# Second half of a four-layer network on one core: four attentions of layer 2 ahead of the first of layer 3, other planned times for the networks' steps, another buffer for the last residual rows

## The reference, cut to what matters

```
x += attn0(norm(x), ctx, ctx, causal)      ; x += norm(x) @ sign(W)
x += attn1(norm(x), ctx, ctx, causal)      ; x += mixture(norm(x))      # 16 experts, top 2, and 2 shared
x += attn2(ctx, norm(x), mask)             ; x += quantised(norm(x))    # silu(gate)*up, down; ternary weights, 8-bit rows
x += attn3(norm(x), ctx, ctx)              ; x += blocks(norm(x))       # below
blocks(h): 3 times  h = lin(gelu(norm(lin(h)) * g + b)) + h
```

## Time and profile before

| | us |
|---|---|
| median of 3 runs | 1590.66 (1587.65 to 1593.19) |
| the profiled execution | 1588.46 |
| its span, first to last instruction | 1586.6 |
| TensorE busy in the span | 1236.1 (78%) |
| VectorE busy | 970.9 (61%) |
| ScalarE busy | 834.0 (53%) |
| GpSimd busy | 434.1 (27%) |
| mean granted TensorE clock | 0.892 of 2.4 GHz |

### The profile page before, as it was taken

One profiled execution on the slowest core, in us unless ns is written; L12 is line 12 of the kernel. 1 busy time (PEld: TensorE's weight loads), 2 busy tenths in 40 slices (PEclk: granted clock), 3 DMA queues, 4 the chain that ended last, 5 costly groups with the idle time before them and its releaser, 6 DMA issues.

```text
span 1586.6 us, 26659 instructions
## 1 busy us (share of the span) xinstructions
PE 1236.1 (78%) x9430; PEld 903.2 (57%) x9430; DVE 970.9 (61%) x2625; ACT 834.0 (53%) x1554; POOL 434.1 (27%) x943
## 2 busy tenths in 40 slices
PE   2888888888998969777887778678686786866775
PEld 2666676666777857655665545446364563543543
DVE  2556765555555658665666777676676856757521
ACT  3445545443555545444554635657466574755651
POOL 3001131444233372444223143212132121111222
PEclk8899999889999989888999969799898897987886
DMA  8566643345776454342856734332243312333000
GB/s 219 134 140 144 96 94 54 54 68 107 146 176 155 115 111 89 79 74 90 180 136 167 170 103 80 40 55 36 31 67 40 56 28 37 41 53 40 1 7 14
DMA packets 98210, 140.06 MB, mean 88 GB/s; under 512 B 12320, under 2 KB 79520, under 8 KB 98080
## 3 DMA queue, kind: packets, MB, share of 16 engines
q1 hardware_dynamic: 90048, 105.58, 36.2%
q0 software_dynamic: 8032, 32.78, 7.6%
HBM read 65.43 MB, written 22.54 MB: 55 GB/s over the span
## 4 chain that ended last, share of the span: by engine, by line
PE 42%; DVE 21%; ACT 13%; POOL 10%; issue 8%; DMA 5%; SPq 1%; ACTq 0%; DVEq 0%; POOLq 0%
PE ps L845 12%; PE ps L959 4%; PE ps L853 4%; PE ps L1049 3%; PE ps L867 3%; PE ps L887 3%; DVE bn L1328 3%; DVE neg_max L1448 2%; POOL rstd L1759 2%; PE ps L837 2%; ACT xn L1181 2%; PE ps L1015 2%; DMA x_rows<-xn,dest 2%; ACT probs L1224 1%; ACT L1311 1%
## 5 line engine op out<-in xcount | busy, mean ns | idle before, releaser
L1224 ACT ACTIVATE probs<-ps 128x384 f32<-128x384 f32 (+1 forms) x512 | 274.2, 542 | 308.9 <-PE ps L890 110.7
L867 PE MATMUL ps<-k_st,q_st 96*128 96x256 bf16 (+1 forms) x1024 | 231.0, 278 | 44.2 <-issue 14.5
L1448 DVE TENSOR_REDUCE neg_max<-ps 128x2 f32<-128x512 f32 x256 | 172.7, 682 | 138.6 <-PE ps L867 81.0
L1756 POOL TENSOR_SCALAR var_eps<-mv 128x2 f32<-128x2 f32 x112 | 25.9, 232 | 845.4 <-DVE mv L1331 842.4
L887 PE MATMUL ps<-q_st,k_st 104*128 104x256 bf16 (+1 forms) x1024 | 229.3, 277 | 21.2 <-ACT q_st L1236 17.7
L1445 DVE TENSOR_REDUCE tri<-ps 128x3 f32<-128x384 f32 x256 | 139.7, 552 | 154.8 <-PE ps L870 153.3
L1236 ACT ACTIVATE q_st<-ps 8x1024 bf16<-8x1024 f32 x128 | 130.2, 1017 | 52.8 <-PE ps L941 50.0
L959 PE MATMUL ps<-probs,v 128*32 128x256 f32 (+1 forms) x2048 | 137.9, 391 | 22.3 <-ACT probs L1224 20.8
L887 PEld LDWEIGHTS ps<-q_st,k_st 104*128 104x128 bf16 x1024 | 103.3, 104 | 66.9 <-ACT q_st L1236 25.2
L867 PEld LDWEIGHTS ps<-k_st,q_st 96*128 96x128 bf16 x1024 | 106.1, 105 | 61.5 <-issue 30.5
L870 PE MATMUL ps<-diag_s,ident_b 128*128 128x128 bf16 x512 | 107.5, 232 | 0.0
(11 more groups left out here) (245 smaller groups left out, 2695.9 us busy)
## 6 DMA issues: line engine op xcount, KB each, us to landing
k_st<-parts SPq DMA_DIRECT2D x192, 128.0 KB
q_st<-parts SPq DMA_DIRECT2D x192, 128.0 KB, 6.8
x_rows<-wo SPq DMA_DIRECT2D x10, 768.0 KB, 8.6
ctx_t<-in_ctx_t SPq DMA_DIRECT2D x16, 256.0 KB, 7.3
ring<-x_rows SPq DMA_DIRECT2D x31, 128.0 KB, 3.5
y_rows<-ring SPq DMA_DIRECT2D x31, 128.0 KB, 3.2
xn_t<-x_rows SPq DMA_DIRECT2D x31, 128.0 KB, 3.8
y_rows<-vec SPq DMA_DIRECT2D x31, 128.0 KB, 3.8
```

Of the source, the lines that this page charges most:

```text
L867: last = mm(t[:, c0:c0 + n], head(q_st, r, h, KROWS, j * P, P), head(k_st, r, h, KROWS, 0, n), start=True, stop=L == 3)
L1224: nc.scalar.activation(probs[:, (hg % 2) * HPG + h4, 0:width], tile_of(key)[:, 0:width], ACT.Exp, scale=SCALE).then_inc(*tile_drained(key))
L1448: V.tensor_reduce(neg_max[:, hg, h4, :], tile_of(key).rearrange("p (j t) -> p j t", j=SJ), AX.X, ALU.max, negate=True).then_inc(*tile_drai ...
```

## The change

1. `interleave(2, 3, 4)`: the second half becomes (2,0) (2,1) (2,2) (2,3) (3,0) (2,4) (3,1) (2,5) (3,2) (2,6) (3,3) (2,7) (3,4) (3,5) (3,6) (3,7). Layer 3 of batch b starts at least four slots after layer 2 of b; before it was three for batches 0 and 7.
2. In the lanes of the second half the offsets are longer: the norm 3.0/4.8/5.8 becomes 4.0/6.6/7.6, a hidden step 8.0 becomes 12.0, a block 18.6 becomes 24.0. `TIME` stays at 42.
3. The lane of the queries of layer 2 starts 1.65 slots ahead of its attention and not 2.
4. The expert tiles of the second group are planned 2.8 apart and not 3.2, so `LOW_AT` and what hangs on it move earlier; the lora weights come after mask 4 and not after mask 3.
5. The contexts of batches 4 to 7 for layer 2 are loaded at a planned time 4.0 into the slot before layer 3 of b - 4.
6. The residual rows of batches 6 and 7 are kept in `stage`, the masks' buffer, loaded once the last mask is made; the alternate y buffers go to batches 5 and 7.

```diff
-HALVES = (list(FIRST), interleave(2, 3))
+HALVES = (list(FIRST), interleave(2, 3, 4))
-TILE_STEP = (3.5, 3.2)
+TILE_STEP = (3.5, 2.8)
+LORA_AT = max(LOW_AT, START[2, 2] + TIME[1] + 2.0) + 2.0
 def norm(part, p, b, t):
+    wait = (3.0, 4.8, 5.8) if p[1] in "01" else (4.0, 6.6, 7.6)
-NORM = 7.0
-OUT = 12.4
+NORM = (7.0, 9.6)
+OUT = (12.4, 13.6)
 def project(part, L, b):
+    wait = (1.4, 2.6, 5.0) if L < 2 else (1.4, 3.6, 6.0)
 def loads_second(part, b):
-    yield START[2, b] - 3.0 * TIME[1]
+    yield START[2, b] - 3.0 * TIME[1] if b < 4 else START[3, b - 4] - TIME[1] + 4.0
 def masks_second(part, b):
-    t = 50.0 + 20.0 * b if b < 2 else max(j - 1.65 * T, START[2, b - 2] + T + 2.0)
-    if b > 3:
-        t = max(t, LOW_AT + 56.0)
+    t = 50.0 + 20.0 * b if b < 2 else START[2, b - 2] + T + 2.0
+    if b > 4:
+        t = max(j - 1.65 * T, t, LORA_AT + 60.0)
 def query_second(part, b):
-    t = START[2, b] - 2 * TIME[1]
+    t = START[2, b] - 1.65 * TIME[1]
-    yield t + 9.4
+    yield t + 12.0
     part.token_bias("q", b)
-    yield t + 13.4
+    yield t + 17.0
     part.apply("q", b)
 def between_second(part, b):
-    yield t + 8.8
+    yield t + 11.4
     part.quantised(b)
...
-        T, s = b * SJ + a, t + 11.2 + 8.0 * a
+        T, s = b * SJ + a, t + 14.4 + 12.0 * a
-            yield s + 2.6 * c
+            yield s + 4.0 * c
             part.hidden(T, c)
...
-        yield s + 2.8
+        yield s + 4.0
         part.down(T)
...
-    t += 35.4
+    t = max(t + 48.0, k - 3.0)
     yield t
     part.ln("l3a", b)
...
 def after_second(part, b):
-    t = START[3, b] + TIME[1] + 6.6
+    t = START[3, b] + TIME[1] + 7.2
-        s = t + NORM + 18.6 * n
+        s = t + NORM[1] + 24.0 * n
...
-        yield s + 6.2
+        yield s + 7.4
         part.apply(("y", n), b)
-        yield s + 8.0
+        yield s + 10.4
         part.block_turn(n, b)
-        yield s + 9.2
+        yield s + 11.4
         part.block_gelu(n, b)
-        yield s + 12.4
+        yield s + 16.0
         part.block_out(n, b)
-        yield s + 14.8
+        yield s + 18.4
         part.block_add(n, b)
-            yield s + 16.0
+            yield s + 20.6
             part.h_turn(n + 1, b)
...
         def y_set(b):
-            return y_sets[1 if b == B - 2 else 0]
+            return y_sets[1 if b in (B - 3, B - 1) else 0]
         def h_of(b):
-            return ctx_n[:, b % 3, :, :]
+            if b < B - 2:
+                return ctx_n[:, b % 3, :, :]
+            return stage[:, (b - B + 2) * SJ * D:(b - B + 3) * SJ * D].rearrange("p (a d) -> p a d", a=SJ)
...
                 def ctx_load(b):
-                    if b > 2:
+                    if b == B - 2:
+                        sp.wait_ge(*mask_ready.at((B - 1, 1)))
+                    elif 2 < b < B - 2:
                         wait_drained(sp, ("z", NBLK - 1, b - 3))
                 def mask_load(b):
-                    elif b == NB:
+                    elif b == NB + 1:
                         wait_drained(sp, ("lora", 2 * NBLK - 1))
                 def lora_load(n):
-                        sp.wait_ge(*mask_ready.at((NB - 1, 1)))
+                        sp.wait_ge(*mask_ready.at((NB, 1)))
```

More of the change, by code:

```diff
@@ L181, in norm @@
 def norm(part, p, b, t):
+    wait = (3.0, 4.8, 5.8) if p[1] in "01" else (4.0, 6.6, 7.6)
     yield t
     part.ln(p, b)
-    yield t + 3.0
+    yield t + wait[0]
     part.apply(p, b)
-    yield t + 4.8
+    yield t + wait[1]
     part.turn(p, b)
-    yield t + 5.8
+    yield t + wait[2]
     part.turned(p, b)
-NORM = 7.0
-OUT = 12.4
+NORM = (7.0, 9.6)
+OUT = (12.4, 13.6)
 def before_first(part, b):
@@ L208, in project @@
     t = START[L, b] + time_of(L) + 6.2
+    wait = (1.4, 2.6, 5.0) if L < 2 else (1.4, 3.6, 6.0)
     yield t
     part.project_in(L, b)
-    yield t + 1.4
+    yield t + wait[0]
     part.projected(L, b)
-    yield t + 2.6
+    yield t + wait[1]
     part.project_out(L, b)
-    yield t + 5.0
+    yield t + wait[2]
     part.project_add(L, b)
 def between_first(part, b):
-    t = START[0, b] + TIME[0] + OUT
+    t = START[0, b] + TIME[0] + OUT[0]
     yield from project(part, 0, b)
     yield from norm(part, "l0f", b, t)
-    yield t + NORM
+    yield t + NORM[0]
     part.ffn0(b)
-    yield t + NORM + 2.4
+    yield t + NORM[0] + 2.4
     part.ffn0_add(b)
-    yield from norm(part, "l1a", b, t + NORM + 3.2)
+    yield from norm(part, "l1a", b, t + NORM[0] + 3.2)
     yield from stacks(part, 1, b)
 def after_first(part, b):
-    t = START[1, b] + TIME[0] + OUT
+    t = START[1, b] + TIME[0] + OUT[0]
     yield from project(part, 1, b)
     yield from norm(part, "l1f", b, t)
-    t += NORM
+    t += NORM[0]
     yield t
@@ L262, in shared_experts @@
 def shared_experts(part, b):
[L264 removed]
+    s = START[1, b] + TIME[0] + OUT[0] + NORM[0] + 2.0
     yield s
@@ L448, in between_second @@
         part.down_copy(T)
-        yield s + 2.8
+        yield s + 4.0
         part.down(T)
-        yield s + 4.2
+        yield s + 5.4
         part.down_add(T)
-    t += 35.4
+    t = max(t + 48.0, k - 3.0)
     yield t
     part.ln("l3a", b)
-    yield t + 3.0
+    yield t + 4.0
     part.apply("l3a", b)
-    yield max(k + 0.6, t + 3.2)
+    yield k + 0.6
     part.k_hi(3, b)
-    yield max(k + 1.8, t + 3.6)
+    yield k + 1.8
     part.k_rest(3, b)
-    yield max(k + 4.6, t + 4.8)
+    yield max(k + 4.6, t + 6.6)
     part.turn("l3a", b)
-    yield max(k + 5.8, t + 5.8)
+    yield max(k + 5.8, t + 7.6)
     part.q_hi(3, b)
-    yield max(k + 6.8, t + 6.8)
+    yield max(k + 7.2, t + 9.0)
     part.q_rest(3, b)
-    yield max(k + 9.0, t + 9.0)
+    yield max(k + 9.4, t + 11.2)
     part.v_take(3, b)
 def after_second(part, b):
-    t = START[3, b] + TIME[1] + 6.6
+    t = START[3, b] + TIME[1] + 7.2
     yield from norm(part, "l3f", b, t)
     for n in range(NBLK):
-        s = t + NORM + 18.6 * n
+        s = t + NORM[1] + 24.0 * n
         yield s
@@ L747, in build @@
         ctx_in = [signal(f"ctx_in{r}", 16) for r in range(4)]
-        ctxn_in = [signal(f"ctxn_in{r}", 16) for r in range(3)]
+        ctxn_in = [signal(f"ctxn_in{r}", 16) for r in range(4)]
         mask_in = signal("mask_in", 16)
@@ L1965, in ctx_load @@
                         wait_drained(sp, ("v", 1, B - 1))
-                    if b > 2:
+                    if b == B - 2:
+                        sp.wait_ge(*mask_ready.at((B - 1, 1)))
+                    elif 2 < b < B - 2:
                         wait_drained(sp, ("z", NBLK - 1, b - 3))
-                    sp.dma_start(h_of(b).rearrange("p a d -> p (a d)"), ctx_d[b]).then_inc(*ctxn_in[b % 3].step(b))
+                    sp.dma_start(h_of(b).rearrange("p a d -> p (a d)"), ctx_d[b]).then_inc(*ctxn_in[b % 4].step(b))
                 def mask_load(b):
```

30 lines of the change are left out of this document (15 added, 15 removed).

## The result

The changed kernel takes 1539.91 us (median of 4 runs, 1533.54 to 1542.88) against 1590.29 for the kernel before. The ratio is 0.9677, 95% interval 0.9643 to 0.9712. Forecast were 1557 us, range 1530 to 1597: the direction is right and the gain was 50 us for 33. The profiled execution of the changed kernel took 1542.88 us, span 1541.1, so 45.5 us of span are to be found. Lines of the code stand six further down (L845 is now L851, and so on).

What follows compares the result with a forecast made beforehand. No engine was full; waits between in-order queues, at steps of the second half's network lanes, were taken as the bound. 1588.5 profiled - 35.6 (lanes) + 2 (tail) = 1554.9, median 2.2 above: 1557 us, range 1530 to 1597.

Steps and rivals of the forecast that it cites:

- The lanes: Second half: longer offsets between the networks' dependent steps fill TensorE's gaps; -35.6 us, bounds zero to -70.
- the cap: VectorE's share of 0.742 in slot (3,0), the most of any slot, taken as what the new order reaches.
- the sum of gaps: TensorE gaps that longer offsets would remove: 10.2 us per slot with the quantised network, 3.8 per slot with layer 2's tokens.
- Rival (b): TensorE's clock comes back as well in five slots with the quantised network, 5.7 us more each: 1529 us; chance 0.13.
- the split: Gain divided by the gaps each lane owns: blocks some 8.7 us of 14.0 a pair, quantised network and preparation the rest.
- Four attentions first: Stretch (2,1) to (3,0): same work in another order, a denser slot (2,3) paid back later; 0, bounds -12 to +17 us.
- Contexts just in time: Context loads of batches 4 to 7 wait behind key stacks with 5 us of room; cost 0, if late +20 us.
- rows in the masks' buffer: Residual rows of batches 6 and 7 load without waiting for block 3 of earlier batches; 0, between -2 and +2 us.
- The tail: After the last exponential: some half block more of batch 6 lies beside batch 7; +2 us, bounds -3 and +8.
- (c): Second half: the gaps only move to another late queue, or room before layer 3 was never short; 1590 us, chance 0.13.
- (d): Quantised network's slots: hidden steps meet the batch's last block on VectorE and shared banks, +41 us: 1598; chance 0.19.
- the signs: Trace checks: right if quantised network's slots take 46 to 49 us; wrong if old-size gaps remain at L845, L887 or L1088.

## Why the prediction was right, and where its sizes were off

**What bounds it.** Right: no engine's work, but TensorE's waits at steps of the networks' lanes. Busy times stayed and the idle time went.

**The lanes, -35.6 us.** The mechanism is right: with the order undone and the offsets kept the gain is 2.9%, with the offsets undone and the order kept it is -0.8%. The term was undersized. The sixteen slots gave 836.1 - 788.6 = 47.5 us, between the term and its bound of -70. The premise that fell is the cap, the VectorE share 0.742 of slot (3,0): slot (3,3) reaches 32.84/38 = 0.864, and over three whole pairs the run with the offsets alone reaches 205.66/268 = 0.767. The highest share that a trace shows was a highest share so far and no limit. Three pairs of the same work gave 26.3 us, 8.8 each, where the cap gave 7.6 (5.3 + 2.3) and the sum of gaps 14.0. So the cap was too low and the gap sum too high, and the cap was nearer.

The clock came back in part only. Rival (b) had priced it at 5.7 us a slot with the quantised network, so 5.7 a pair. The trace shows 0.80 to 0.96 in slot (3,3), but in three pairs of the same work TensorE's busy time fell by 0.6 us, by 2.6 with the offsets alone, and by 7.5 between the two kernels with four attentions first: 0.2 to 2.5 us a pair.

The Trainium skill, page "TensorE: Matmul & The Clock Gate", section "HAM oscillation — how this bites in real kernels", has the rule that the prediction cites, on waits that bring the array back to half rate. The trace agrees in its direction: 0.96 for 0.80 with the waits gone.

**Which offsets.** Wrong in the split. By the gaps that a lane owns the blocks should have held 8.7 of 14.0 a pair and the quantised lane 5.3; put back, they cost 5.7 and 6.7 a pair, and 17 and 45 us in all. What the split left out is the first six and the last four slots, where no gap had been read and where the quantised lane costs over 20 us more. Nor is a gap's length what an edit at it is worth: with the 4.10 us gone in the old order the kernel gains 15 us, the down product's gap of 1.28 stayed at 1.21 and yet the down steps moved closer cost 24 us, and the start of the hidden steps, which owned no gap, is worth 14. Of the 28 us of the two distances together, the wait of 3.96 us behind the hidden rows is a part; what carries the rest stays open.

**Four attentions first, 0.** Right within what can be told: 0.9677 against 0.9707 with the offsets, 1.0084 without them, so -5 to +13 us, with all the edits that are no offsets in it. The dense slot (2,3) came a little under what was worked out: 52.17 us of VectorE and 72.6 us long, where 55 to 61 and 74 to 82 were given; (3,0) behind it fell from 64.9 to 40.8. Its longest TensorE wait, 6.35 us at 909.33, stands before the context's product, but is no late context. VectorE's add that frees the bank stood behind the merges of batch 4, which waited for their fetches:

```profile
904.46 0.48 DVE L1583 SCALAR_TENSOR_TENSOR x<-xn_t,weight,x 128x256 f32<-128x256 f32 x1 [2.17 <-DMA xn_t<-y_rows,dest]
...
907.16 0.48 DVE L1583 SCALAR_TENSOR_TENSOR x<-xn_t,weight,x 128x256 f32<-128x256 f32 x1 [2.21 <-DMA xn_t<-y_rows,dest]
```

```profile
909.33 3.75 PE L851 MATMUL ps<-w,ctx_t 128*128 128x256 f32 x8 [6.35 <-DVE x L1369]
```

**Contexts just in time, rows in the masks' buffer, 0.** The load went out at 1183.52, behind the key stacks, and the next product of a context ran at 1194.03, 10.5 us later, for 5 us of room beyond the landing in the forecast. In the whole second half no wait before a context product is put down to a DMA. These edits weren't undone one by one: with four attentions ahead the old ones wait on each other. That they cost nothing is read from the trace, not shown by a run.

```profile
1179.69 3.79 SPq L1958 DMA_DIRECT2D k_st<-parts  x6
1183.52 0.60 SPq L1925 DMA_DIRECT2D ctx_t<-in_ctx_t  x1
```

**The tail, +2.** It was +3.6, inside the bounds. In the kernel with the old blocks' lane it is 58.5 us, as before, so the longer blocks are what lengthens it. Of it 2 us lie ahead of batch 7's first block, which stands behind an output product of batch 6 and begins 13.6 us after the last exponential (1479.0) for 11.6 (1539.70 - 1528.1); the blocks then follow each other by 15.65 and 15.02 us for the 14.06 and 15.13 of the earlier trace rows, another 1.5:

```profile
1489.19 3.62 PE L851 MATMUL ps<-w,ring 128*128 128x256 f32 x8
1492.60 2.64 PE L851 MATMUL ps<-w,xn_t 128*128 128x256 f32 x8
...
1508.25 1.89 PE L851 MATMUL ps<-w,xn_t 128*128 128x256 f32 x8
...
1523.27 3.78 PE L851 MATMUL ps<-w,xn_t 128*128 128x256 f32 x8 [0.69 <-ACT xn_t L1144]
```

**The rivals and the signs.** (c) is out. (d), the jam of the hidden steps with the blocks' last block once both lie at 28, did not come: the slots are shorter, and the longest wait behind the hidden rows in the pair shown is 1.84 us. To begin at 23.6 with the last block still at 22.8 to 41.2 costs 14 us, so later was right. That the two lanes overlap at all was not undone by a run. Of the signs, the slots with the quantised network are shorter than forecast, 38 to 43 us for 46 to 49, and (2,1) is not shorter (62.4 us for 62.1); one sign of being wrong stands too, a wait of 2.62 us at L851.

## What to carry to other kernels

In a kernel whose queues follow one written plan, offsets that are shorter than the real latencies make TensorE wait at the network's steps; lengthening them was worth 3%, and what the order with more room adds is within the noise. Do not cap the price of such an edit by the highest share that an engine has shown, and do not take the sum of gaps for it either: here they gave 35.6 and 70 us, and 47.5 came. Before you compare two windows of different orders, count that they hold the same work: six slots against six slots showed 8 us less busy time, and it was work that lay elsewhere. And try each lane's offsets by themselves, in both directions, over the whole kernel: the gaps of one pair pointed to the wrong lane, and a second round of covering gaps gained nothing.

## What the runs showed of the hardware that was not expected

The granted clock can carry more of a difference than the waits that come with it. With the down steps 8.0 apart three pairs took 273 us for 264: idle time 52.3 for 50.3 us, TensorE's busy time 220.73 for 213.68 with the same products, clock 0.86 for 0.90. It is the exception among these runs: with the quantised lane put back, 17.8 of 20 us are idle time at the same clock of 0.90.
